# The count plane of a dense adjacency build as a bf16 product beside a float32 product

## The reference, cut to what matters

```python
# L0: softmax over the edges of a source, then a weighted sum
p = ex / seg_sum[src];  h = segment_sum(norm_h[src] * p[:, None], dst)
# L1 (twice): attention per edge, softmax over the edges of a destination
ex = exp(leaky_relu(a_src[src] + a_dst[dst], 0.2) - m[dst])
out = segment_sum((ex / denom[dst])[:, :, None] * h[src], dst)
# L2 (three times): degree-normed sum
agg = segment_sum((dinv[src] * edge_weight * dinv[dst])[:, None] * xl[src], dst)
```

## Time and profile before

| | |
|---|---|
| runs | 6582.43, 6587.01, 6589.16 us |
| the profiled execution | 6587.06 us, with a span of 6585.7 us |
| TensorE busy over the span | 4445.8 us |
| VectorE (DVE) busy | 3996.1 us |
| ScalarE (ACT) busy | 1574.3 us |
| GpSimd (POOL) busy | 1578.2 us |
| mean DMA rate | 111 GB/s |

### The profile page before, as it was taken

How to read it: one execution, slowest core, us unless ns; L and a number is a source line. 1 busy time by engine, 2 the same in 40 slices (tenths; PEclk the granted TensorE clock), 3 DMA queues, 4 the chain that set the end, 5 groups by cost and what they waited for, 6 DMA issues and landing times. The chain is left out here.

```text
span 6585.7 us, 52701 instructions
## 1 busy us (share of the span) xinstructions
PE 4445.8 (68%) x15996; PEld 2523.9 (38%) x15998; DVE 3996.1 (61%) x4480; ACT 1574.3 (24%) x1840; POOL 1578.2 (24%) x1634
## 2 busy tenths in 40 slices
PE   3611102259998999998888797788878887444443
PEld 1100000035554554894333387333334443333333
DVE  6621213878887876898999889899980011211112
ACT  0100000002689201444555400355540003000000
POOL 1677777300000000000000000000000002777776
PEclk9999999999999999557999955899989998555555
DMA  3100101072578215563333266233326666222222
GB/s 59 20 14 12 16 11 18 18 284 72 152 208 239 77 75 191 147 178 100 113 113 113 89 185 184 83 113 113 113 81 258 249 233 180 52 53 53 53 53 56
DMA packets 624209, 729.35 MB, mean 111 GB/s; under 512 B 96361, under 2 KB 556423, under 8 KB 604725
## 3 DMA queue, kind: packets, MB, share of 16 engines
q1 hardware_dynamic: 571812, 669.98, 33.0%
q0 software_dynamic: 52144, 56.00, 3.7%
HBM read 542.42 MB, written 183.38 MB: 110 GB/s over the span
## 5 line engine op out<-in xcount | busy, mean ns | idle before, releaser
L1100 POOL DMA_INDIRECT ring<-rel_dram,rel_pair x806 | 765.6, 950 | 4577.8 <-POOLq L68 4332.5
L898 PE MATMUL total<-to,from 128*128 128x384 f32 x2816 | 939.9, 492 | 33.5 <-issue 27.7
L1645 PE MATMUL sums<-acc,hw 128*64 128x392 f32 x2144 | 742.9, 502 | 138.0 <-DVE acc L1579 137.6
L1180 PE MATMUL total<-ring,onehot 128*128 128x128 f32 x1612 | 415.4, 439 | 579.0 <-DMA ring<-rel_dram,rel_pair 578.6
L517 POOL DMA_INDIRECT cells_dram<-rec,place x742 | 729.8, 984 | 226.1 <-issue 219.1
L898 PEld LDWEIGHTS total<-to,from 128*128 128x128 f32 x2816 | 523.6, 190 | 450.1 <-issue 123.4
L1135 DVE TENSOR_SCALAR onehot<-iota,loc_pair 128x128 f32<-128x128 f32 x806 | 182.9, 291 | 812.0 <-PE total L1180 812.0
L706 PE MATMUL alike<-right,left 18*128 18x512 bf16 x352 | 174.1, 616 | 734.2 <-DVE top L666 629.8
L1180 PEld LDWEIGHTS total<-ring,onehot 128*128 128x128 f32 x1612 | 357.3, 325 | 637.0 <-issue 636.9
L1645 PEld LDWEIGHTS sums<-acc,hw 128*64 128x64 f32 x2144 | 268.6, 137 | 578.8 <-issue 304.5
L1645 PE MATMUL sums<-p,hw 128*64 128x392 f32 x1056 | 375.8, 499 | 62.7 <-DVE p L1579 62.5
(11 more groups left out here) (346 smaller groups left out, 6040.9 us busy)
## 6 DMA issues: line engine op xcount, KB each, us to landing
strip<-ac_dram SPq DMA_DIRECT2D x100, 1600.0 KB, 6.8
count<-ac_dram SPq DMA_DIRECT2D x200, 784.0 KB, 4.2
ac_dram<-stage SPq DMA_DIRECT2D x625, 192.0 KB, 2.5
lo_row<-lo_dram SPq DMA_DIRECT2D x44, 1024.0 KB, 6.9
h<-ac_dram SPq DMA_DIRECT2D x26, 1600.0 KB, 8.3
acc<-ac_dram SPq DMA_DIRECT2D x24, 1600.0 KB, 9.4
rel_dram<-rows SPq DMA_DIRECT2D x25, 1024.0 KB, 5.4
mask_dram<-mask SPq DMA_DIRECT2D x25, 800.0 KB, 5.5
```

The costliest lines, as they stand in the source:

```text
L898: nc.tensor.matmul(spots[:, at(spot), 0:WIDTH].rearrange("p o n -> p (o n)"), from_[:, n % RING, u, :], to[:, n % RING, u, :, :].rearrange ...
L1100: pool.indirect_dma_start(ring[:, j % SLOTS, :], None, m.rel_dram[:, :], bass.IndirectOffsetOnAxis(ap=m.rel_pair[:, j:j + 1], axis=0)).the ...
L1180: last = nc.tensor.matmul(total[:, at(col, D)], onehot[:, j % U, :], ring[:, j % SLOTS, :], start=False, stop=False, skip_group_check=True)
L1645: last = nc.tensor.matmul(psum[kk * 2 * HC:(kk + 1) * 2 * HC, banks(i) + q, 0:PIECE], hw[:, t, k, :], p[n % 3][:, piece], start=t == 0, st ...
```

## The change

The count plane is made of zeros and ones alone, and so are the one-hots of the sources: bf16 holds both without loss. The change takes the count plane out of the float32 product.

```diff
-        from_, to = sb("from", [P, RING, BB, P]), sb("to", [P, RING, BB, PLANES, P])
+        from_, to = sb("from", [P, RING, BB, P]), sb("to", [P, RING, BB, 2, P])
+        from_b, to_b = sb("from_b", [P, RING, BB, P], BF16), sb("to_b", [P, RING, BB, P], BF16)
...
-                v.tensor_tensor(to[:, b, :, 1, :], mid(m.iota[:, :], BB), bc(m.ends_col[:, 1, cols], P), ALU.is_equal).then_inc(marked, 1)
                 v.tensor_tensor(from_[:, b, :, :], mid(m.iota[:, :], BB), bc(m.ends_col[:, 0, cols], P), ALU.is_equal).then_inc(marked, 1)
-                dve.wait_ge(marked, 4 * n + 1)
-                v.tensor_tensor(to[:, b, :, 0, :], to[:, b, :, 1, :], bc(m.w_col[:, cols], P), ALU.mult).then_inc(marked, 1)
-                v.tensor_tensor(to[:, b, :, 2, :], to[:, b, :, 1, :], bc(m.share_col[:, cols], P), ALU.mult).then_inc(marked, 1)
+                v.tensor_tensor(to_b[:, b, :, :], mid(m.iota[:, :], BB), bc(m.ends_col[:, 1, cols], P), ALU.is_equal).then_inc(marked, 1)
+                dve.wait_ge(marked, 5 * n + 2)
+                v.tensor_tensor(to[:, b, :, 0, :], to_b[:, b, :, :], bc(m.w_col[:, cols], P), ALU.mult).then_inc(marked, 1)
+                v.tensor_tensor(to[:, b, :, 1, :], to_b[:, b, :, :], bc(m.share_col[:, cols], P), ALU.mult).then_inc(marked, 1)
+                v.tensor_copy(from_b[:, b, :, :].rearrange("p u d -> p (u d)"), from_[:, b, :, :].rearrange("p u d -> p (u d)")).then_inc(marked, 1)
...
-                    pe.wait_ge(marked, 4 * (n + 1))
+                    pe.wait_ge(marked, 5 * (n + 1))
...
-                    nc.tensor.matmul(spots[:, at(spot), 0:WIDTH].rearrange("p o n -> p (o n)"), from_[:, n % RING, u, :],
-                                     to[:, n % RING, u, :, :].rearrange("p k d -> p (k d)"), start=False, stop=False, skip_group_check=True).then_inc(summed, 1)
+                    nc.tensor.matmul(spots[:, at(spot), 0:2 * P].rearrange("p o n -> p (o n)"), from_[:, n % RING, u, :],
+                                     to[:, n % RING, u, :, :].rearrange("p k d -> p (k d)"), start=False, stop=False, skip_group_check=True)
+                    nc.tensor.matmul(spots[:, at(spot), 2 * P:WIDTH].rearrange("p o n -> p (o n)"), from_b[:, n % RING, u, :],
+                                     to_b[:, n % RING, u, :], start=False, stop=False, skip_group_check=True).then_inc(summed, 1)
...
-                sp.dma_start(strip[:, t % L0_STRIPS, :], m.ac_dram[t][:, 2, :]).then_inc(strip_in[t % L0_STRIPS], 16)
+                sp.dma_start(strip[:, t % L0_STRIPS, :], m.ac_dram[t][:, 1, :]).then_inc(strip_in[t % L0_STRIPS], 16)
...
-            kind, into = (1, m.cnt) if first else (0, m.deg)
+            kind, into = (2, m.cnt) if first else (0, m.deg)
...
-                sp.dma_start(count[:, n % 2, :], m.ac_dram[n % NT][:, 1, h * HALF:(h + 1) * HALF]).then_inc(count_in[n % 2], 16)
+                sp.dma_start(count[:, n % 2, :], m.ac_dram[n % NT][:, 2, h * HALF:(h + 1) * HALF]).then_inc(count_in[n % 2], 16)
```

More of the change, by code:

```diff
@@ L863, in _ @@
             dve.wait_ge(cleared, 2)
-            v.tensor_copy(fresh[:, 2, 1, :], m.ident[:, :])
+            v.tensor_copy(fresh[:, 2, 2, :], m.ident[:, :])
             dve.wait_ge(zeroed, 1)
-            v.tensor_copy(total[:, P:2 * P], m.ident[:, :]).then_inc(cleared, 1)
+            v.tensor_copy(total[:, 2 * P:3 * P], m.ident[:, :]).then_inc(cleared, 1)
             v.sem_inc(freed, SPOTS)
```

## The result

The kernel after takes 6608.06 us (median; 6604.27 to 6613.75), the kernel before, beside it on the same chip, 6586.24 us (6580.85 to 6591.09). The ratio is 1.0032 [1.0023, 1.0041]: **slower by 21.8 us**, 0.32%. That lies inside the range given, but it is not the likeliest case, which was 4 us and no measurable change. The prediction called 0.2% the least that can be told from no change; by that bound the outcome is "slower", which it gave 0.26.

What follows compares the result with a forecast made beforehand. TensorE was taken to bound the first and last stretches, ScalarE the middle. With DVE bounding at 5.27 us a turn, 129.4 t - 678.5 gave +4 us on 6587: 6591 us, range 6576 to 6612.

Steps and rivals of the forecast that it cites:

- dearer copy: Rival: DVE's bf16 copy runs at strided L1190's pace, 5.56 us a turn, +41 us, 6628; 0.18 together with lost overlap.
- lost overlap: Rival variant: DVE loses 0.085 us of overlap at the copy, giving 6602 us; 0.18 together with the dear copy.
- DVE becomes the bound: In `dense`, DVE's four operations plus wait and copy make 5.27 us a turn, almost TensorE's present pace.
- The wait directly ahead: DVE's wait `5 * n + 2` for the operation directly ahead loses the overlap: +0.12 us a turn.
- Mixed types: Rival: DVE operations touching `to_b` run two numbers a cycle, sum -109 us, 6478; 0.10 shared with some cost counted twice.
- TensorE's chunk: Two float32 passes of 256 columns, one bf16 pass and the rest of a weight load: 0.55 us a chunk.
- loads hide behind the passes: Rival denied this: loads exposed at type changes, TensorE's turn 5.9 us, +98 us, 6685; chance 0.05.
- the clock: Rival: TensorE's pauses drop it to the lower clock level; half the turns there cost +175 us; chance 0.03.
- a turn 4.4 us in place of 5.16: TensorE's turn after the change, from 0.55 us a chunk, where it takes 5.16 us now.
- some 0.9 us of waiting for the cast a turn: Sign expected in the profile after: TensorE's groups wait some 0.9 us for DVE's cast in each turn.
- The head start of the ring: The full ring's lead, unused today as 10.9 us from DVE's last operation to TensorE's end, is spent in the last stretch.
- TensorE and DVE cannot shorten the middle stretch: From 1900 to 2185.6 us ScalarE bounds, busy 267.87 of 285.6 us, so the stretch keeps its length.

Runs made afterwards that it cites:

- experiment 4: Kernel after with destinations marked ahead of sources, so the wait no longer asks for the operation directly ahead: 6600.48 us, ratio 1.0029.
- experiment 7: Kernel after, complete, with the table word loaded without bounds and the freed-spot count through one register operation: 6581.15 us, ratio 1.0001.
- experiment 10: Kernel before with only the lighter table word load (no bounds, one register operation for the freed-spot count): 6576.63 us, ratio 0.9988.
- experiment 1: Kernel after without the copy to bf16, the bf16 tile cleared once, four marks a turn: 6601.27 us, ratio 1.003.
- (2): The kernel of experiment 1 with one unused table word load added for each group of four chunks: 6800.0 us, ratio 1.0332.
- experiment 3: Kernel after with one float32 matmul of 384 columns again, keeping DVE's new order, near wait and a cast nobody reads: 6589.51 us, ratio 1.0014.
- experiment 5: Kernel before with five always-met waits, each with an empty instruction, added to TensorE's program per group of four chunks: 6604.37 us, ratio 1.0037.

## Why the prediction was right in its range, and where its working failed

**What was luck.** The 6608 us lie inside the range because it reached to 6612, and that part was there for a dearer copy or a lost overlap behind it. Neither came. What did come, the sequencer, is in no term and among no rival.

**What held.** DVE becomes the bound at 5.27 us a turn: measured 5.266 and 5.267. The cast: 685 ns against 694 taken from L639; the dear copy did not happen. The wait directly ahead costs 0.12 us: experiment 4's turns are 5.14. Mixed types are not fast (1217 to 1225 ns). TensorE's chunk: 0.54 us against 0.55; loads hide behind the passes also where the types change, and that rival is out. So is the clock: chunks 0.54 us apart are the upper level, in spite of the pauses.

Both rules that the prediction quotes from the Trainium skill are quoted by half. The section on the TRN2 errata (VectorE: DVE Perf Modes) says itself that its 58 cycles fall short of a measured copy; the cast here is 685 ns, not 594. And "The mechanism" (TensorE: Matmul & The Clock Gate, Part 3) also names loads into a background weight buffer as ones that can be pulled ahead of running matmuls; only its narrower sentence, on row groups, is contradicted by the loads hidden here.

**The sum from these terms held as well, where nothing else was in the way.** Experiments 7 and 10 differ by this change alone, both with a light sequencer. Against the kernel before beside each they are 0.8 and 7.7 us faster, so the change costs 6.9 us by the medians, and 5.9 in `dense` (974.16 against 968.23), where the sum said +4 (129.4 x 5.27 - 678.5 is 3.4; the prediction wrote 4). Each of the two ratios is known to some 6 us, so it is `dense` that bears this out.

**What failed: "a turn 4.4 us in place of 5.16".** I multiplied 0.55 us by eight and took for granted that TensorE always has the next matmul at hand. The term that limits the group was never costed, and so stood at nothing: the sequencer's operations between matmuls, which are in the trace of before as well. The forecast sign "some 0.9 us of waiting for the cast a turn" did not show either: 6.2 us of TensorE's idle time are put down to the cast in all. A turn of TensorE's side is 5.1 to 5.2 us when quiet. It was planned to be 0.9 us below DVE; it was 0.1. Three things follow, and they make up the difference between +4 and +20.7:

- In turns 40 to 88 it loses to DVE: +10.0 us over 48 turns of 5.267. There the table load itself gets longer while ScalarE and the stores are at work. The load's records in after (min/median/max ns), the stretch from 1675 us, then the last one:

```profile
L878 PEldq TENSOR_LOAD <-spot_row x32: 299/606/625, 1675.0 to 1763.9; - x32
...
L878 PEldq TENSOR_LOAD <-spot_row x65: 297/301/311, 2231.4 to 2398.2; - x65
```

  A group grows by just what its load grows. In experiment 1, the groups of turns 144 to 160 take 2.604 us with a mean load of 0.302, those of turns 32 to 48 take 2.801 with 0.499. The kernel before has the long loads in the same place, where 10 to 17 passes of backlog hide them:

```profile
L876 PEldq TENSOR_LOAD <-spot_row x35: 341/522/775, 1675.5 to 1764.4; - x35
```

- The end: I took 4.4 us for TensorE's last turn and it is 7.6 behind DVE's last operation; by the table, "end" is 13.5 us where experiment 7, with the sequencer light, has 11.1: +2.4.
- The middle stretch. The head start of the ring should be spent there: what the other rows and the forecast's +4 leave for turns 88 to 136 is 297.6 us. It is 301.9: +4.3. Experiment 7 has 294.7, some 4 us of which are the lighter words' own gain (experiment 10). That the rest is the sequencer's catching up after each wait for a bank fits, but was not measured by itself.

10.0 + 2.4 + 4.3 = 16.7, the 20.7 less the 4.

That the sequencer is the cause is shown from four sides: the copy gone and nothing gained (1), a load added and all of it visible (2), the slowdown made in the old kernel with waits alone (5), and the slowdown gone with a lighter load (7). The pause behind the table load in each group is the same thing seen in the trace. Alone, DVE's added work costs 7.6 us (experiment 3), and the sequencer with the near wait but without the copy 19.3 us (experiment 1); together they cost 21.8, for what they hold up overlaps. Still open is why a table load takes 0.4 to 0.6 us instead of 0.3 while ScalarE and the stores are busy; no run separated the two.

My statement that TensorE and DVE cannot shorten the middle stretch was also too strong. Less work of the sequencer does, by some 4 us (turns 88 to 136: 303.8 before, 299.8 in experiment 10).

## What to carry to other kernels

Where matmuls have addresses from registers, count the sequencer's operations for each of them as one more engine, and look how far it is ahead before you shorten or split what it feeds: here it was 17 passes ahead, and one address operation of 0.124 us more a chunk, together with shorter passes, took all of it. When a change moves the bound from one engine to the next with 0.1 us a turn between them, every engine near that pace needs its price, the one that issues too. A row with much idle time put down to "issue" while its consumer waits for it is a hint of this, and no more: the kernel before has 27.7 us of it, 27.4 in the middle stretch, and experiment 5 has no more (27.6) with the sequencer at the bound. And moving a small copy to an idle engine pays only if that engine does not slow the busy one.

## What the hardware showed that I had not expected

- A satisfied wait with its no-operation costs 0.106 us of TensorE's sequencer; a register operation 0.097, an address operation 0.124, a table word with its bounds 0.64 us from start to next.
- TensorE starts a chunk 0.1 us behind its address operation when nothing is in reserve.
- The table load is 0.30 us in quiet stretches and 0.6 us (median) from 1675 to 1764 us, in one and the same kernel.
- GpSimd's cast of 128 x 1024 from float32 to bf16 takes 1.97 us against DVE's 0.69, and raises a DVE multiplication beside it from 1.22 to 2.05 us.
